# Two-layer decoder block on one core: the softmax reciprocals spread over partitions through a bf16 turn and a selection matrix instead of fp32 broadcast products

## The reference, cut to what matters

```python
def attn_block(xq, ctx, Wq, Wk, Wv, Wo, bo, pe_q, pe_k, mask):
    ...
    sim = jnp.einsum('bhid,bhjd->bhij', q, k)          # 8 heads of 64
    a = jax.nn.softmax(sim, axis=-1)
    out = jnp.einsum('bhij,bhjd->bhid', a, v)
    return out.reshape(b, n, INNER) @ Wo + bo
for l in range(DEPTH):                                  # 4 layers
    x = attn_block(h, h, sWq[l], ...) + x               # h: rmsnorm of x
    x = attn_block(h, chunked_seq, cWq[l], ...) + x     # 154 keys
    x = gelu(h @ fW1[l] + fb1[l]) @ fW2[l] + fb2[l] + x
```

## Time and profile before

| | |
|---|---|
| median of 3 runs | 1398.38 us (1397.79 to 1398.71) |
| the profiled execution's own time | 1397.06 us |
| its span, first to last instruction | 1395.0 us |
| TensorE busy | 1255.1 us, 90% |
| VectorE, ScalarE, GpSimd busy | 710.3, 742.3, 399.2 us |
| the four layers | about 85 to 1000 us of the span |

### The profile page before, as it was taken

One profiled execution on the slowest core, in us unless ns is written; L12 is line 12 of the kernel. 1 busy time (PEld: TensorE's weight loads), 2 busy tenths in 40 slices (PEclk: granted clock), 3 DMA queues, 4 the chain that ended last, 5 costly groups with the idle time before them and its releaser, 6 DMA issues.

```text
span 1395.0 us, 21171 instructions
## 1 busy us (share of the span) xinstructions
PE 1255.1 (90%) x7630; PEld 754.9 (54%) x7630; DVE 710.3 (51%) x2061; ACT 742.3 (53%) x1897; POOL 399.2 (29%) x379
## 2 busy tenths in 40 slices
PE   4499998989999898999989899998759995898898
PEld 2244555554455464445556445465449993454687
DVE  6665554356555435555543555644334115675454
ACT  1176666637666654765664576665323444364332
POOL 1343332254332316324321633422220101110100
PEclk8599999999999999999999999999969998899799
DMA  4000000010000001000000000000011100000010
GB/s 142 0 1 0 24 1 9 23 29 2 0 24 8 2 24 29 1 1 23 9 24 8 16 1 1 16 2 1 1 56 31 38 25 0 1 1 1 9 35 24
DMA packets 27096, 22.49 MB, mean 16 GB/s; under 512 B 4342, under 2 KB 22131, under 8 KB 26995
## 3 DMA queue, kind: packets, MB, share of 16 engines
q1 hardware_dynamic: 26995, 21.14, 5.2%
HBM read 20.60 MB, written 0.52 MB: 15 GB/s over the span
## 4 chain that ended last, share of the span: by engine, by line
PE 83%; DVE 9%; POOL 3%; ACT 2%; issue 1%; DMA 0%; SPq 0%; DVEq 0%; POOLq 0%
PE bank L1455 13%; PE bank L1414 10%; PE bank L1433 8%; PE bank L1474 7%; PE bank L1486 6%; PE bank L1466 4%; PE bank L1631 4%; PE bank L1430 4%; PE bank L1407 3%; PE bank L1479 3%; PE bank L1569 2%; PE bank L1571 2%; PE bank L1570 2%; PE bank L1847 2%; PE bank L1538 1%; PE bank L1735 1%
## 5 line engine op out<-in xcount | busy, mean ns | idle before, releaser
L798 DVE CUSTOM_DVE_ANT_0 bank<-bank,maskrow 128x512 f32<-128x512 f32 x256 | 172.3, 715 | 151.5 <-PE bank L1414 151.3
L1179 ACT ACTIVATE probs<-bank,tops 128x512 f32<-128x512 f32 x256 | 174.3, 685 | 128.0 <-DVE tops L798 127.9
L612 POOL TENSOR_TENSOR rot<-rot,sin 128x512 f32<-128x512 f32 (+1 forms) x112 | 134.3, 1199 | 376.2 <-DVE rot L787 376.2
L1191 ACT ACTIVATE KA<-bank 128x512 f32<-128x512 f32 x256 | 139.1, 600 | 31.8 <-PE bank L1433 31.8
L1414 PE MATMUL bank<-QA 64*128 64x512 f32 x512 | 146.6, 653 | 7.7 <-DVE rot L787 7.0
L1433 PEld LDWEIGHTS bank<-ident,probs 128*128 128x128 f32 x1024 | 116.8, 141 | 54.4 <-issue 45.5
L1433 PE MATMUL bank<-ident,probs 128*128 128x128 f32 x1024 | 134.7, 274 | 2.3 <-ACT Vs L1156 2.3
L1455 PE MATMUL bank<-KA,Vs 128*64 128x512 f32 x512 | 135.4, 615 | 0.0
L1175 ACT ACTIVATE probs<-bank,tops 128x154 f32<-128x154 f32 x256 | 95.5, 383 | 57.1 <-DVE tops L795 56.6
L614 POOL TENSOR_TENSOR QA<-rot 128x512 f32<-128x512 f32 x96 | 121.8, 1269 | 7.5
L786 DVE TENSOR_TENSOR rot<-bank,cos 128x512 f32<-128x512 f32 (+1 forms) x112 | 73.8, 659 | 74.3 <-PE bank L1474 55.6
(11 more groups left out here) (250 smaller groups left out, 2191.5 us busy)
## 6 DMA issues: line engine op xcount, KB each, us to landing
f<-in_fW SPq DMA_DIRECT2D x8, 256.0 KB, 3.1
Vc<-in_wup SPq DMA_DIRECT2D x8, 192.0 KB, 2.5
wk<-in_sWk SPq DMA_DIRECT2D x4, 256.0 KB, 2.8
wq<-in_sWq SPq DMA_DIRECT2D x4, 256.0 KB, 3.2
wv<-in_sWv SPq DMA_DIRECT2D x4, 256.0 KB, 4.1
wo<-in_sWo SPq DMA_DIRECT2D x4, 256.0 KB, 3.7
ck<-in_cWk SPq DMA_DIRECT2D x4, 256.0 KB, 2.7
cv<-in_cWv SPq DMA_DIRECT2D x4, 256.0 KB, 3.1
```

The costliest lines, as they stand in the source:

```text
L612: g.tensor_tensor(turned, turned, tab, ALU.mult).then_inc(q.pool_step, 1)
L798: v.tensor_tensor_reduce(bank[i][:, :], bank[i][:, :], maskrow[:, u.b * S:(u.b + 1) * S], -SCALE, 3.0e38, ALU.add, ALU.min, tops[:, g % 4, ...
L1179: c.activation(to, bank[i][:, :], ACT.Exp, bias=tops[:, g % 4, e, 0:1], scale=-1.0, accum_out=sums[:, n, k, e:e + 1]).then_inc(q.probs_rea ...
L1191: c.activation(turned_self(u)[:, half, :, k * P:(k + 1) * P], bank[4 + half][:, :].rearrange("p (c t) -> p c t", t=P), ACT.Copy).then_inc( ...
```

## The change

The reciprocals of a unit (128 queries on partitions, 8 columns: 4 tiles by 2 heads) are split by VectorE into three bf16 parts (high, middle, low) of 8 columns each, 24 columns in all. `sum_rows` has TensorE turn these 24 columns into 24 rows of 128 in bank 7, `rows_out` has VectorE copy them to recr, and `spread` makes four bf16 products (24 rows deep, 128 by 128) with the matrix `pick`, whose ones select the three parts of a tile and a head; the fp32 accumulation adds the parts. `pick` comes by one more DMA (24 by 512, fp32) and is cast once. In VectorE's step `reciprocals` is moved from ahead of `top` to behind it.

```diff
@@ DVE
                 n = step.unit.n
-                v.reciprocal(recs[:, n % 4, :, :], sums[:, n % 4, :, :]).then_inc(q.rec_ready, 1)
+                r = recs[:, n % 4, :, :].rearrange("p t e -> p (t e)")
+                link(v.reciprocal(recs[:, n % 4, :, :], sums[:, n % 4, :, :]))
+                link(v.tensor_copy(recp[:, n % 4, 0, :], r))
+                link(v.tensor_tensor(rest[:, 0, :], r, recp[:, n % 4, 0, :], ALU.subtract))
+                link(v.tensor_copy(recp[:, n % 4, 1, :], rest[:, 0, :]))
+                v.tensor_tensor(recp[:, n % 4, 2, :], rest[:, 0, :], recp[:, n % 4, 1, :], ALU.subtract).then_inc(q.rec_ready, 1)
+
+            def rows_out(u):
+                dve.wait_ge(q.rows_full, u.n + 1)
+                v.tensor_copy(recr[:, u.n % 2, :], bank[7][0:3 * 2 * TB, 0:P // 2].bitcast(BF16)).then_inc(q.rows_ready, 1)
...
                 elif p.what == "out":
                     reciprocals(p.step)
+                    rows_out(p.step.unit)
...
                     if step.unit:
-                        if step.before and step.before.k == step.before.unit.tiles - 1:
-                            reciprocals(step.before)
                         if step.dve:
                             turned_out(step)
                         if step.after and not step.late:
                             for e in range(2):
                                 top(step.after, e)
+                        if step.before and step.before.k == step.before.unit.tiles - 1:
+                            reciprocals(step.before)
+                    for u in step.spread:
+                        rows_out(u)
                     for u in step.done:
                         normalise(u)
@@ PE
-            def spread(u):
+            def sum_rows(u):
 
                 pe.wait_ge(q.rec_ready, u.n + 1)
                 free(7)
+                turn(bank[7][0:3 * 2 * TB, 0:P // 2].bitcast(BF16), recp[:, u.n % 4, :, :].rearrange("p a c -> p (a c)"),
+                     identb[:, :]).then_inc(q.rows_full, 1)
+                lend([7], q.rows_ready)
+
+            def spread(u):
+
+                pe.wait_ge(q.rows_ready, u.n + 1)
+                free(7)
                 for t in range(TB):
-                    for e in range(2):
-                        ins = mm(bank[7][rows_of(e), t * P:(t + 1) * P], recs[:, u.n % 4, t, e:e + 1].broadcast_to([P, DH]),
-                                 ident[:, :], start=True, stop=True)
+                    ins = mm(bank[7][:, t * P:(t + 1) * P], pick[:, t * P:(t + 1) * P], recr[:, u.n % 2, :], start=True, stop=True)
                 ins.then_inc(q.spread_full, 1)
                 lend([7], q.spread_ready)
...
+                elif p.what == "out":
+                    sum_rows(p.step.unit)
...
                     for u, k in step.weigh:
                         weigh(u, k)
+                    for u in step.spread:
+                        sum_rows(u)
                     for p in step.pieces:
                         if p.early:
                             piece(p)
@@ SP and the start of DVE
                 sp.dma_start(b2e[:, :], a["b2"]).then_inc(q.small_in, 16)
+            sp.dma_start(recT[0:3 * 2 * TB, 0, :], a["pick"]).then_inc(q.small_in, 16)
...
+            v.tensor_copy(pick[:, :], recT[0:3 * 2 * TB, 0, :])
```

More of the change, by code:

```diff
@@ L243, in decoder @@
         recs = sb("recs", [P, 4, TB, 2])
+        recp = sb("recp", [P, 4, 3, 2 * TB], BF16)
+        rest = sb("rest", [P, 2, 2 * TB])
+        recr = sb("recr", [3 * 2 * TB, 2, P], BF16)
+        pick = sb("pick", [3 * 2 * TB, S], BF16)
         recT = sb("recT", [P, 2, S])
@@ L387, in decoder @@
             spread_ready = sem("spread_ready")
+            rows_full = sem("rows_full")
+            rows_ready = sem("rows_ready")
             mv_ready = sem("mv_ready")
@@ L1092, in _ @@
             v.tensor_copy(ctxT[:, 0:B * C], bank[2][:, 0:B * C]).then_inc(q.ctx_ready, 1)
-            dve.wait_ge(q.small_in, see.next(q.small_in, 128))
+            dve.wait_ge(q.small_in, see.next(q.small_in, 144))
+            v.tensor_copy(pick[:, :], recT[0:3 * 2 * TB, 0, :])
             dve.wait_ge(q.w_early, see.next(q.w_early, 32))
@@ L1583, in _ @@
             pe.wait_ge(q.w_early, see.next(q.w_early, 32))
-            pe.wait_ge(q.small_in, see.next(q.small_in, 128))
+            pe.wait_ge(q.small_in, see.next(q.small_in, 144))
             for b in range(B):
@@ L1902 @@
     arrays["cos"], arrays["sin"] = np.concatenate([one, one]), np.concatenate([two, two])
+    turned = np.arange(3 * 2 * TB)[:, None] % (2 * TB) == 2 * (np.arange(S) // P) + np.arange(S) % P // DH
+    arrays["pick"] = turned.astype(np.float32)
     arrays["tri8"] = np.tril(np.ones((E, E), np.float32))
```

## The result

The changed kernel takes 1535.85 us (median of 4 runs, 1530.62 to 1537.49), the kernel before 1398.09 (4 runs, 1397.36 to 1398.71): a ratio of 1.0979, 95% interval 1.0952 to 1.1006. It is slower by 138 us. Forecast was slower by some 41 us, 1439, with a range up to 1453. The sign was right, the size more than three times too small.

The account below looks back on a forecast made before the run. TensorE, busy for 90%, was taken as the bound. Added waits of 10.6 us a layer, 42 over four, plus 0.4 for the DMA, gave 1397.06 + 42.8 = 1439.9, rounded down to 1439; range 1416 to 1453.

Parts of the forecast that it names:

- That VectorE's place in TensorE's list decides, not the work removed: Each spread gains two VectorE round trips in TensorE's list, blocking later turns, scores and products; 10.6 us a layer.
- The prices of the instructions: New spread path: chain 0.99 us, turn's product 0.22, copy 0.29, four products until next block 0.40; old spread 1.02.
- The self steps: Six self steps s6 to s26 of a layer: next block starts +0.22 us later each, +1.3 a layer.
- my sum: Added waits over all steps: 10.6 us a layer, 42 for four layers, 42.8 in the total.
- each of four small linked instructions 0.17: VectorE's chain behind the reciprocals: 0.17 us per instruction plus a 0.03 gap, so 0.99 with reciprocals, against 0.19 before.
- My bound of 0.20 for a small instruction: Upper price of one small VectorE instruction, 0.20 us, bounding the chain from reciprocals to last part at 1.12.
- The clock falls (0.05 within slower): Rival, chance 0.05: TensorE idle stretches up to 2.5 us lower the clock; 9 us per 1% half clock, over 1450.
- The forecast's parts of the profile: Signs expected: spread products under 25 us, TensorE busy share down 3 to 5 points, new waits for VectorE.
- the 2 us at END: At a layer's END, up0 starts about 2 us later because the last unit's spread blocks TensorE ahead of it.
- the 0.3 to 0.5 in self steps: Self steps: TensorE's new wait for VectorE's row copy and last part, 0.3 to 0.5 us.
- over 1.5 in s34: Step s34, where a residual holds VectorE: new TensorE wait for copied rows and last part, over 1.5 us.
- The reciprocals' move behind top as the cause of the waits in s36, s40 and s42: Cross steps: reciprocals, moved behind the tops, delay TensorE; +1.22 us in s36, +1.1 in s40, +1.2 in s42.

Follow-up runs that it names:

- the chain alone: Kernel before, fp32 products kept, with VectorE's reciprocals behind top and four linked split instructions whose results are never read; 1472.86 us, ratio 1.0511.

## Why the prediction was right or wrong

- *That VectorE's place in TensorE's list decides, not the work removed*: right. The same split, turn and products give 1.0979 in one order and 0.9878 in another (the second also has the casts as reductions, worth 19 us in the first).
- *The prices of the instructions*: right or a little high. The turn took 0.227 (0.22 forecast), the copy 0.21 (0.29), the stretch from the products' start to the next turn 0.31 (0.40), an undisturbed link of the chain 0.20. The self steps came out at +0.04 instead of +0.22. Over 56 places that is some 10 us less than my sum. In s34 the prediction also took 0.86 for tops whose row says 0.81, which is 0.4 us in the whole.
- *"each of four small linked instructions 0.17"*: this term was mis-sized wherever GpSimd was at work. The casts and subtractions of the chain took 71.7 us where 4 x 64 x 0.17 = 43.5 were priced, 28 us more. About 19 of them lie in the cross steps, where TensorE waits: s38's chain took 3.0 instead of 0.99. The other 9 or 10 are the first cast at 0.65 in five self steps of each layer, where it does not. I took the price from L846 and L816, which have one SBUF input and no cast, and looked for wait time on VectorE where the rows show it as duration. My bound of 0.20 for a small instruction could not hold this. With both corrections the sum is 42.8 - 10 + 19 = 52 us, and the table has 51 for the waits less the saving. So the part of the forecast that was worked out was some 9 us too low, with two errors that partly cancel.
- *"The clock falls (0.05 within slower)"*: the step that failed. The forecast of 1439 puts this term at nothing. I had listed the mechanism, and priced it per percent of time without asking how much of the time it would take; for the small chance the prediction gives no reason. The kernel before kept 1.00 beside waits such as the 1.52 of s38, and even beside one of 2.3 at the start of the second layer. The runs showed 0.90 over the layers, 89 us more for the same other work of TensorE, and giving TensorE work in the waits brought 73 of the 138 us back. The rival was right in kind and far too cheap ("over 1450"), and its chance was too low.
- *The forecast's parts of the profile*: the 2 us at END, the 0.3 to 0.5 in self steps (0.48) and the idle time "over 1.5 in s34" (3.02) were there; s36 had 0.87 for the parts and 0.40 for the copy, under the 1.5 named for it, though near the +1.22 of its own sum; the four products took 26.9 us, where under 25 was named; TensorE's share did fall, from 90% to 86%, but its busy time rose, which I had not foreseen, and which is the sign by which a slow clock is told from a wait.
- *The reciprocals' move behind top as the cause of the waits in s36, s40 and s42*: right as far as shown. With it undone, 50 us came back, though the casts then stalled more; in the table some 12 of them are idle time and 41 half clock.

The sign of the forecast came from the right cause, the waits. What stays open: how the 63 us between the changed kernel and the one with the chain alone split between turn, copy and END; and why the half clock comes behind some waits and not behind others of the same length, as behind the 3.02 us of s34 in the first and in the third layer of the kernel with the chain alone.

## What to carry to other kernels

Before a product is made cheaper by a detour over another engine, place the detour: in an in-order list, the round trip ate all that the cheaper products saved even in the best steps (1.02 us against 0.98), unless other work of the waiting engine stood between (0.49). Price an idle stretch on TensorE twice, once as waiting and once as half clock on what follows, and test the second by filling the wait with useless products. Put small VectorE instructions that have two SBUF inputs, or cast from SBUF, where GpSimd is idle, or write the cast as a reduction over one element.

## What the runs showed of the hardware that I had not expected

- A wait of 3.02 us for TensorE in s34 was followed by 1.2 GHz (a turn of 1.97 instead of 1.09 us), and useless products in the wait, fp32 or bf16, mostly prevented such falls: the mean clock went from 0.894 to 0.946 and 0.941.
- The same wait of 3.02 us, at the same place of two layers of one kernel, was followed by 1.2 GHz once (a turn of 1.97 us) and by 2.4 GHz once (1.09).
- A cast of eight elements a partition took up to 1.26 us, ending within 0.03 us of GpSimd's instruction; the same cast as a maximum over one element took 0.16 in all 64 places.
